# Attention maps of a differential-attention layer: both sides of a head in one pass, operands in four row groups, results joined in SBUF

## The reference

```
q = q.reshape(B, N, H, 2, HD)      # B = 2, N = 1024, H = 16, HD = 4
k = k.reshape(B, N, H, 2, HD)
v = v.reshape(B, N, H, 2 * HD)
def sdpa(qi, ki):
    s = jnp.einsum('bnhd,bmhd->bhnm', qi, ki) * scale
    p = jax.nn.softmax(s, axis=-1)
    return jnp.einsum('bhnm,bmhe->bhne', p, v)
a1 = sdpa(q[:, :, :, 0], k[:, :, :, 0])
a2 = sdpa(q[:, :, :, 1], k[:, :, :, 1])
o = a1 - lam * a2
o = _rms_norm(o, sub_norm_w, EPS) * (1.0 - LAMBDA_INIT)
```

## Time and profile before

| | |
|---|---|
| median of three runs | 3904.56 us (3898.9 to 3905.77) |
| span of the profiled execution | 3896.6 us |
| TensorE busy, whole span | 3299.6 us (85%) |
| VectorE busy | 3022.0 us (78%) |
| ScalarE busy | 2012.2 us (52%) |
| POOL busy | 1097.2 us (28%) |
| granted TensorE clock, mean | 0.950 |
| `attention_maps`, from its first instruction to that of the join | 73.30 to 1112.65 us |

### The profile page before, as it was taken

The page is one execution under the profiler, slowest core; times in us unless marked ns, Lnnn a source line. Parts: engine busy times, 40 slices in busy tenths (PEclk is TensorE's granted clock), DMA queues, the critical chain, the costliest instruction groups (busy, mean ns, idle before and its releaser), DMA issues. The chain is left out here.

```text
span 3896.6 us, 71287 instructions
## 1 busy us (share of the span) xinstructions
PE 3299.6 (85%) x25164; PEld 1850.2 (47%) x25164; DVE 3022.0 (78%) x3833; ACT 2012.2 (52%) x2780; POOL 1097.2 (28%) x610
## 2 busy tenths in 40 slices
PE   5999999999965788878787878887878787878997
PEld 2222222222234555555555555555555555547886
DVE  3777777777734989898989898989898988955664
ACT  1455555555532656665666565656556565631111
POOL 2000000000012545354535453544353444410000
PEclk6999999999976999999999999999999999988998
DMA  3000000000021100110010001000100110010000
GB/s 108 12 15 16 14 14 15 15 15 14 15 92 38 41 22 28 30 42 23 28 45 27 22 27 45 27 21 23 50 27 17 33 28 22 22 33 1 0 0 28
DMA packets 70709, 107.04 MB, mean 27 GB/s; under 512 B 26790, under 2 KB 41012, under 8 KB 69684
## 3 DMA queue, kind: packets, MB, share of 16 engines
q1 hardware_dynamic: 69716, 104.37, 9.3%
q10 hardware_dynamic: 864, 0.79, 0.1%
HBM read 38.79 MB, written 15.73 MB: 14 GB/s over the span
## 5 line engine op out<-in xcount | busy, mean ns | idle before, releaser
L918 DVE TENSOR_REDUCE a_part_max<-a_ps_max 128x1 f32<-128x512 f32 x1024 | 683.1, 690 | 290.5 <-PE a_ps_max L840 288.6
L816 ACT ACTIVATE a_expT<-a_ps_scoresT 128x1024 f32<-128x1024 f32 x512 | 516.8, 1024 | 315.6 <-PE a_ps_scoresT L852 310.0
L861 PE MATMUL a_ps_out<-a_expT,a_v_op 128*32 128x512 f32 x2048 | 537.6, 605 | 0.6 <-issue 0.5
L1204 POOL TENSOR_TENSOR b_turned_q<-b_rot_q,b_turned_q 128x1024 f32<-128x1024 f32 x96 | 226.8, 2363 | 925.8 <-DVE b_turned_q L1540 925.8
L1618 DVE STREAM_TRANSPOSE b_probsT<-b_probs 32x1024 f32<-32x1024 f32 x384 | 474.6, 1236 | 14.1 <-POOL b_probs L1220 2.0
L840 PE MATMUL a_ps_max<-a_k_op,a_q_op 96*128 96x512 bf16 x1024 | 401.5, 392 | 25.0 <-DMA a_k_op<-terms_k 21.1
L840 PEld LDWEIGHTS a_ps_max<-a_k_op,a_q_op 96*128 96x128 bf16 x1024 | 98.3, 96 | 515.5 <-DVE a_part_max L918 428.5
L1420 PE MATMUL b_psD<-b_probsT,b_v 128*64 128x128 f32 x3072 | 337.9, 278 | 5.8 <-DVE b_probsT L1618 5.8
L1421 PE MATMUL b_psD<-b_probsT,b_v_back 128*64 128x128 f32 x3072 | 332.9, 274 | 0.0
L1435 PE MATMUL b_psD<-b_w_qkv,b_xs 128*128 (+1 forms) x384 | 215.1, 648 | 116.7 <-ACT b_outT L1284 116.7
L1370 PE MATMUL b_psQ<-b_w_qkv,b_xs 128*128 (+1 forms) x384 | 194.2, 629 | 138.6 <-DVE b_xs L1498 138.6
(11 more groups left out here) (292 smaller groups left out, 6259.2 us busy)
## 6 DMA issues: line engine op xcount, KB each, us to landing
b_v_back<-b_v SPq DMA_DIRECT2D x96, 384.0 KB, 3.5
b_v_back<-b_v SPq DMA_DIRECT2D x96, 128.0 KB, 3.4
b_w_qkv<-L_ffn_Wqkv SPq DMA_DIRECT2D x6, 1536.0 KB
sums<-a_outT SPq DMA_DIRECT2D x512, 16.0 KB
j_got<-sums SPq DMA_DIRECT2D x16, 512.0 KB
a_q_op<-terms_q SPq DMA_DIRECT2D x64, 48.0 KB
a_k_op<-terms_k SPq DMA_DIRECT2D x64, 48.0 KB
b_w_o<-L_ffn_Wo SPq DMA_DIRECT2D x6, 512.0 KB
```

The lines of the kernel that those rows point to most:

```text
L816: act.activation(expT[kt % RING][:], ps_scoresT[kt % 2][:], ACT.Exp, scale=SCALE_A).then_inc(exp_ready, 1)
L861: last_mm = pe.matmul(ps_out[lo:lo + 32, :], v_op[(u // 2) % 2][:, kt, :], expT[kt % RING][:, 512 * half:512 * half + 512], start=(kt < 2) ...
L918: dve.tensor_reduce(part_max[:, qt, half:half + 1], ps_max[half][:], AX.X, ALU.max).then_inc(max_taken, 1)
L1204: pool.tensor_tensor(turned[:], rot[:], turned[:], ALU.add).then_inc(added, 1)
```

## The change

- Both sides of a head, which share the value, are done together: 32 pairs instead of 64 maps, with 8 steps a pair. All loops over pairs are written out.
- `q_op` and `k_op` hold both sides twice, at rows 0, 32, 64 and 96: row group 2 x side + copy. A matmul reads only the 24 (maxima) or 26 (scores) rows of one group; the half of the queries or keys that it makes picks the copy. The row maximum lies right behind the terms, so a group is 26 rows. No row is zero, and the only clearing left is one memset of ones for each `k_op`. A pair's operands are eight DMAs (were four for two maps).
- A maximum tile is 1024 wide: two matmuls of two row groups fill the two banks of a `ps_max`, and VectorE reduces both at once, with the sign turned, into a column of `minus_max`. TensorE turns that tile in fp32 into a corner of `ps_max1`; VectorE takes the high and the low part straight from there (`row_out`). Eight DMAs (were four for two maps) send the rows.
- The transposed scores go to a ring of three banks. Exponentials are 1024 and 512 wide in turn (banks 0 and 1, then bank 2) and write to a ring of 18 halves.
- The weighing of a step is four matmuls, one for each side and half, in the four column strips, with the same weights straight from `v_aug`, which is now 32 wide for each head. They accumulate over all eight steps, so there are no partial sums. POOL copies nothing.
- The copy of the sums stands on ScalarE behind the exponential that takes in the second step's last half; SP moves it to the SBUF tensor `joined` (eight DMAs a pair, were sixteen for two maps). `join_maps` reads `joined` where it lies; its loads and additions are gone.

The core of the diff:

```diff
@@ attention_maps, tiles
-        v_op = [sb(f"v_op{i}", [P, TILES_PER_BATCH, 32]) for i in range(2)]
-        expT = [sb(f"expT{i}", [P, N]) for i in range(RING)]
+        expT = sb("expT", [P, SLOTS * 512])
-        ps_max = [pb(f"ps_max{i}", [P, 512]) for i in range(2)]
-        ps_scoresT = [pb(f"ps_scoresT{i}", [P, N]) for i in range(2)]
+        ps_max = [pb(f"ps_max{i}", [P, N]) for i in range(2)]
+        ps_scoresT = pb("ps_scoresT", [P, 3 * 512])
         ps_out = pb("ps_out", [P, 512])
+        ps_row = ps_max[1][0:UNITS, 0:P]
+        def group(side, copy):
+            return 32 * (2 * side + copy)
@@ ScalarE
+            for e in range(EXPS):
+                first = 3 * (e // 2) + 2 * (e % 2)
+                size = min(2 - e % 2, HALVES * PAIRS_A - first)
+                end = first + size
+                act.wait_ge(scoresT_ready, end)
+                if end > SLOTS:
+                    act.wait_ge(pv_done, (end - 1 - SLOTS) // 4 + 1)
...
+                if end >= HALVES * (copied + 1) + 8:
+                    out_copy(copied)
+                    copied += 1
@@ TensorE, max_scores_of(u): unit u is tile u % 16 // 2 of side u % 2 of pair u // 16
+                if u >= 2:
+                    pe.wait_ge(max_taken, u - 1)
+                if u % UNITS == 1 and p >= 1:
+                    pe.wait_ge(max_lo_ready, p)
                 for half in range(2):
+                    lo = group(side, half)
+                    last_mm = pe.matmul(ps_max[u % 2][:, 512 * half:512 * half + 512], q_op[slot][lo:lo + ROWS, P * qt:P * qt + P],
+                                        k_op[slot][lo:lo + ROWS, 512 * half:512 * half + 512], start=True, stop=True)
+                last_mm.then_inc(max_scores, 1)
+                if u % UNITS == 0 and p >= 1:
+                    turn_row(p - 1)
+            def turn_row(p):
+                pe.wait_ge(max_taken, UNITS * (p + 1))
+                pe.transpose(ps_row, minus_max[p % 2][:], ident[:]).then_inc(row_turned, 1)
@@ TensorE, scores(p, kt, side, place) and weigh(p, kt)
+                    n = HALVES * p + 4 * kt + place + half
+                    lo = group(side, half)
+                    if n >= 3:
+                        pe.wait_ge(exp_ready, exp_of(n - 3) + 1)
+                    pe.matmul(ps_scoresT[:, 512 * (n % 3):512 * (n % 3) + 512], k_op[slot][lo:lo + ROWS + 2, P * kt:P * kt + P],
+                              q_op[slot][lo:lo + ROWS + 2, 512 * half:512 * half + 512], start=True, stop=True).then_inc(scoresT_ready, 1)
...
+                for place, (side, half) in enumerate(((1, 0), (1, 1), (0, 0), (0, 1))):
+                    lo = group(side, half)
+                    at = 512 * ((n + place) % SLOTS)
+                    last_mm = pe.matmul(ps_out[lo:lo + 32, :], v_aug[:, b * T8 + kt, head, :], expT[:, at:at + 512],
+                                        start=(kt == 0), stop=(kt == T8 - 1))
@@ TensorE, the loop
+            for p in range(PAIRS_A):
+                pe.wait_ge(row_in[p % RING], 128 * (p // RING + 1))
                 for kt in range(T8):
+                    u = UNITS * (p + 1) + LEAD + 2 * kt
+                    if u < UNITS * PAIRS_A:
+                        max_scores_of(u)
...
+                    scores(p, kt, 1, 0)
+                    if u < UNITS * PAIRS_A:
+                        max_scores_of(u + 1)
+                    scores(p, kt, 0, 2)
+                    if kt >= 2:
+                        weigh(p, kt - 2)
+                    elif p >= 1:
+                        weigh(p - 1, T8 - 2 + kt)
@@ VectorE
+            def row_out(p):
+                dve.wait_ge(row_turned, p + 1)
...
+                dve.tensor_copy(max_hi[p % 2][:], ps_row).then_inc(max_hi_ready, 1)
+                dve.wait_ge(max_hi_ready, p + 1)
+                dve.tensor_tensor(max_lo[p % 2][:], ps_row, max_hi[p % 2][:], ALU.subtract).then_inc(max_lo_ready, 1)
@@ join_maps
-                dve.tensor_tensor(mean[n % 2][:], numerators[n % 2][:], ps_inv[:], ALU.mult).then_inc(mean_ready, 1)
+                dve.tensor_tensor(mean[n % 2][:], joined[b][:, 0, :, lo:lo + GROUP], ps_inv[:], ALU.mult).then_inc(mean_ready, 1)
@@ build
-            res_a = dict(res, terms_q=terms_q, terms_k=terms_k, sums=sums,
-                         v_aug=sb_a("v_aug", [P, TILES, HEADS_A, 2 * VD_A]), proj_bias=sb_a("proj_bias", [P, 1]),
+            res_a = dict(res, terms_q=terms_q, terms_k=terms_k, joined=[sb_a(f"joined{b}", [P, 2, 2, N]) for b in range(BATCHES)],
+                         v_aug=sb_a("v_aug", [P, TILES, HEADS_A, 32]), proj_bias=sb_a("proj_bias", [P, 1]),
```

More of the change, by code:

```diff
@@ L750, in _ @@
[L750 to L756 removed]
+                            lo = group(side, half) + VD_A * kind
+                            sp.dma_start(joined[b][at:at + VD_A, kind, side, 512 * half:512 * half + 512],
+                                         outT[p % 2][lo:lo + VD_A, :]).then_inc(out_sent[p % 2], 16)
```

318 lines of the change are left out of this document (102 added, 216 removed).

## The result

The changed kernel takes **3947.99 us** (median; 3944.85 to 3949.32), the kernel before, beside it on the same chip, 3903.55 (3898.90 to 3905.77): ratio 1.0114, 95% interval 1.0100 to 1.0129. It is slower by 1.1%, where 3622 us and a faster kernel were forecast. The time lies outside the range, and 20 us from the rival "the clock is not raised" (3968).

What follows compares the result with a forecast made beforehand. TensorE was taken to bound the attention maps, next a loop through ScalarE. The 3896.6 us span less 270.8 for the stage and 12 for join and additions gave 3613.8; with 8.0 from span to median, 3622 us, range 3545 to 3710.

Steps and rivals of the forecast that it cites:

- the clock is not raised: Rival: TensorE, waiting for ScalarE, stays at half clock in the attention maps; 33.5 us a pair, 3968 us; chance 0.06.
- third rival: The rival "the clock is not raised"; argued against because new steps stream about 3.0 of 4.15 us at half clock.
- The rival's sum: Half-clock attention steps of 4.15 us, 3.7 the short one, mean 4.0; 33.5 us a pair, 346 more, 3968 in all.
- Four-strip weighing: Product with the values: four matmuls in four column strips cost what two did, 1.06 us, saving 251 us in all.
- Row groups side by side: Maxima and scores: four matmuls in different row groups run at once, 0.22 us instead of 0.88 one after another.
- Loop through ScalarE: A step's last score waits for an exponential of the same step: 2.79 or 2.37 us, mean 2.65, 21.2 a pair.
- VectorE not the bound: Maximum reductions: two a step need 2.27 us, under the step's 2.65, so VectorE does not set the pace.
- Sixth step: Turning the maxima for the row makes this step of a pair 3.6 us, about 0.9 over the mean.
- The row's DMAs: Eight DMAs deliver the row 9.0 us after the sixth step began, needed at 8.9; a tie, 0.2 us a pair.
- Start: Opening of the attention maps, with less clearing: first maximum matmul at 78.7 us, first scores at 105.9.
- Stage end and join: Last weighing to next stage 5.6 us as before; join's first matmul after about 0.1 instead of 11.1, 12 saved altogether.

Runs made afterwards that it cites:

- e13: Changed kernel plus two 24-row filling matmuls a step in one row group, one after another, ahead of the second maximum tile: 3979.63 us.
- e7: Changed kernel with maximum matmuls reading all 128 rows, nothing added, attention values not the reference's: 3777.05 us.
- e2: Changed kernel plus two 128-row filling matmuls a step, result unread, ahead of the second maximum tile: 3684.62 us.
- e10: Kernel before the change with each exponential done three times, so that TensorE waits for ScalarE with wide operands: 4442.65 us.
- e11: e8 with the last scores of the sixth step ahead of the maximum tile, and wide filling in the last pair too: 3589.84 us.
- e1: Changed kernel plus two narrow pairs of filling matmuls a step, each pair side by side in two row groups: 3819.92 us.
- e6: Changed kernel plus one 128-row filling matmul a step ahead of the second maximum tile: 3707.22 us.
- e8: Changed kernel with exponentials 512 wide throughout and two 128-row filling matmuls a step: 3603.90 us.
- e15: e11 without the two filling matmuls in the sixth step of a pair: 3581.54 us, the best version.
- e3: Changed kernel with every exponential 512 wide instead of 1024 and 512 in turn: 3810.23 us.
- e4: Changed kernel with a step's weighing put between its second maximum tile and its last scores: 4055.13 us.
- e5: Changed kernel plus four narrow pairs of filling matmuls a step, each pair in two row groups: 3958.96 us.
- e14: Changed kernel plus two 128-row filling matmuls a step on a cleared tile of zeros: 3683.89 us.
- e9: Kernel before the change with its maximum matmuls reading 24 rows instead of 96: 4005.75 us.

## Why the prediction was wrong

**The step that failed** is the last argument against the third rival: that at half clock the new steps have TensorE "streaming about 3.0 of 4.15 us", and would therefore be raised where the opening was not. It took for granted that streaming time is what counts. e13 refutes it directly: 97% busy with 24- to 26-row operands beside the weighing, clock 0.50; by the distances of the starts its steps stream for some nine tenths, against 3.0 of 4.15 us in that argument. And the old loop, which I took as evidence that this kind of code holds 1.00, had 96- and 128-row operands in every matmul. The change itself made those of maxima and scores narrow: that it did, and that TensorE waits at the same time, was in the text, each for itself. With wide operands in their place the clock was full (0.99 in e7, 0.96 with wide filling in e2); the exact rule, and how much the waits add to it, stay open. The chance of 0.06 was far too low, and the range should have reached to 3968.

That the Trainium skill's page (TensorE: Matmul & The Clock Gate, section "A second HAM failure mode: psum-queue depth-cycling") warns of short idles between banks was weighed and set aside. As far as the runs go, short idles are neither enough nor needed: e10 waits 0.87 us a step in the mean and cycles its banks, at 1.00, and e13 hardly waits, at 0.50.

**The rival's sum held.** It gave 4.15 us a long step (4.17 in the trace) and 33.5 us a pair (33.2). Of the 20 us between its 3968 and the result, the pairs are 31 x 0.3 = 9, and 8 are the distance of median and span, which the changed kernel doesn't have (span 3947.5).

**Point by point.**
- *Four-strip weighing*: predicted eight records in 1.06 us; 1.07 at full clock (e11, 501.62), 1.94 at half. Right; but at half clock it costs what the old weighing cost at full clock (1.05 us a step of one map).
- *Row groups side by side*: right, four matmuls in 0.62 us against 0.61 for one, and the set holds TensorE for 0.40 us, about as long as one narrow matmul of e13 (0.43). The Trainium skill (same page, section "Measured speedup vs the span model") gives 3.07 times for four row tiles. The trace agrees: four one after another would take 3 x 0.43 + 0.61 = 1.9 us from the first start to the last end, an estimate, against 0.62, which is 3.1 times. The working in the prediction that made this 0.28 us a set at full clock was wrong: the factor holds for the whole length of a set, not for what it adds to a list.
- *Loop through ScalarE*: right. At full clock, in e1, pairs of 22.03 and 23.40 us, against 22.7 predicted. The third of the cycle was at full clock throughout only in runs with wide filling (24.76 in e6, 25.12 in e2), so the mean without filling is at most some 23.4, an estimate that takes it that filling never shortens a pair: 22.7 was 0.7 too low at most.
- *VectorE not the bound*: right in the changed kernel. In e8 it comes close, 533 us busy of 600.
- *Sixth step*: predicted 3.6 at full clock; e11 has 4.14 (498.48 to 502.62), of which 0.53 is filling, and e15, without it, 3.62. The row's DMAs: a tie was predicted. In the changed kernel, at half clock, TensorE never waits for them from 150 to 750 us; in e15, at full clock, it waits some 0.3 us a pair (7.6 us in 600).
- *Start*: the first maxima came at 83.2, not 78.7, the first scores at 110.4, not 105.9. In the other kernels with the same start (e1, e3, e4, e5, e13, e14) the first maxima lie between 78.9 and 83.5, so this term had a spread of 4 us that a single trace doesn't show.
- *Stage end and join*: from the last weighing to the join 8.3 us, not 5.6, because the eight DMAs of a pair take 5.3 us on SP's queue, where those of a map took 2.65; the join's first matmul comes 0.04 us after its start instead of 11.1, and the join is 15.0 us shorter (84.8 to 69.8), 12 predicted. What follows the join is 4.7 us longer, for a cause that stays open.

So the sum of the stage was nearly right for a stage at full clock: with pairs of at most 23.4 us the changed kernel would have taken 3948 - 31 x (33.2 - 23.4) = 3644 us or less, an estimate from the pairs of e1 and e6. The clock cost about 300 us. That time would still have been 22 us above the forecast, but inside its range.

## What to carry to other kernels

Before believing a gain from narrow matmuls (few rows, row groups side by side), ask what clock TensorE will be granted: a stage that runs much of its matmul work over few rows and also waits may stay at half clock, as this one did, and then the best packing loses to the plain one. The test is cheap: put one or two wide matmuls, on zeros if need be, into a bank that is about to be overwritten, at the point where TensorE waits anyway; if the kernel gets faster by more work, the clock was the bound. Take them out again where they stand in a chain (e15), and do not prize TensorE's busy share as such: the run with the highest one was the slowest of the filled ones.

## What the runs showed of the hardware

- TensorE's busy share alone does not tell the granted clock: 97% busy at 0.50 (e13), 71% busy at 1.00 (e10), 86% busy at 0.96 (e2). Between e13 and e2, which fill equally long in the same place, what differs is how many rows the filling reads; zeros do as well as data (e14).
- Neither narrow maxima beside wide scores without waits (e9) nor waits with wide matmuls (e10) lowered the clock (1.00 in both); narrow maxima and scores almost without waits kept it at 0.50 (e13). Which of the two, or how much of each, brings a stage down from full clock is open.
- A change between 24-row and 128-row matmuls of 128 columns costs 0.1 us each way at full clock (e9: 0.32 for 0.22, 0.53 for 0.44).
- Four matmuls in four row groups, two on one operand pair and two on another, start within 0.01 us of each other (508.23 to 508.24 in the changed kernel) and end as closely.
